# Second attention: the scores computed once, scaled by rows and turned, in place of a second pass of scores

## The reference

```python
qkv = data @ W_qkv + b_qkv
q = qkv[:, :, :DIM].reshape(n, l, H, HD)      # k, v alike; H=16, HD=64
scores = jnp.einsum('nqhd,nkhd->nhqk', q, k)
attention = jax.nn.softmax(scores / jnp.sqrt(jnp.float32(HD)), axis=3)
out = jnp.einsum('nhql,nlhd->nqhd', attention, v).reshape(n, l, DIM)
return out @ W_out + b_out
```

## Time and profile before

| | |
|---|---|
| median of 3 runs | 3018.5 us (3016.71 to 3020.96) |
| span of the profiled execution | 3025.9 us (its time beside the span is not recorded) |
| TensorE busy | 2770.4 us (92%) |
| VectorE busy | 2107.9 us (70%) |
| ScalarE busy | 1731.9 us (57%) |
| GpSimd busy | 1752.1 us (58%) |
| chain that ended last | PE 31%; DVE 4%; POOL 4%; issue 4%; ACT 2% |

### The profile page before, as it was taken

One profiled execution on the slowest core, in us unless ns is written; L12 is line 12 of the kernel. 1 busy time (PEld: TensorE's weight loads), 2 busy tenths in 40 slices (PEclk: granted clock), 3 DMA queues, 4 the chain that ended last, 5 costly groups with the idle time before them and its releaser, 6 DMA issues. The chain is left out here.

```text
span 3025.9 us, 50008 instructions
## 1 busy us (share of the span) xinstructions
PE 2770.4 (92%) x17716; PEld 1938.1 (64%) x17716; DVE 2107.9 (70%) x4508; ACT 1731.9 (57%) x3340; POOL 1752.1 (58%) x1540
## 2 busy tenths in 40 slices
PE   7999999999999999989994787999999999999376
PEld 6995565656656565648883674666666666665276
DVE  5667777777777777666776435877877778777632
ACT  5665777776776767676772343544544545445142
POOL 0004989898898989891110573555555555555067
PEclk9999999999999999989996798999999999999588
DMA  3015444444544545420002331000000000000033
GB/s 101 1 58 129 119 117 117 115 114 109 130 106 113 123 106 131 105 71 5 23 15 67 72 60 33 2 5 5 9 5 6 5 9 5 5 6 9 28 84 50
DMA packets 146695, 179.65 MB, mean 59 GB/s; under 512 B 31571, under 2 KB 76176, under 8 KB 145936
## 3 DMA queue, kind: packets, MB, share of 16 engines
q1 hardware_dynamic: 132368, 165.72, 21.7%
q0 software_dynamic: 14080, 10.73, 2.7%
HBM read 56.51 MB, written 17.72 MB: 25 GB/s over the span
## 5 line engine op out<-in xcount | busy, mean ns | idle before, releaser
L1982 POOL TENSOR_TENSOR arena<-arena 128x512 f32<-128x512 f32 x1152 | 1447.0, 1284 | 565.7 <-ACT arena L1325 450.8
L1605 DVE TENSOR_REDUCE top<-psum 128x1 f32<-128x512 f32 x1536 | 974.6, 677 | 196.0 <-PE psum L917 123.6
L1325 ACT ACTIVATE arena<-psum 128x512 f32<-128x512 f32 x1536 | 840.8, 600 | 240.7 <-PE psum L917 141.3
L909 PE MATMUL psum<-stack 96*128 96x512 f32 (+1 forms) x2048 | 627.5, 426 | 16.5 <-ACT arena L1325 9.3
L960 PE MATMUL psum<-arena,values 128*32 128x512 f32 (+1 forms) x3072 | 477.6, 597 | 3.4 <-ACT arena L1325 3.4
L909 PEld LDWEIGHTS psum<-stack 96*128 96x128 f32 (+1 forms) x2048 | 344.0, 191 | 198.1 <-DVE top L1605 87.7
L960 PEld LDWEIGHTS psum<-arena,values 128*32 128x32 f32 (+1 forms) x3072 | 134.0, 119 | 290.0 <-issue 284.8
L917 PE MATMUL psum<-stack 64*128 64x512 f32 x2048 | 292.5, 399 | 11.8 <-DVE top L1605 5.6
L1951 POOL TENSOR_SCALAR rstd<-mv 128x4 f32<-128x4 f32 x56 | 13.0, 233 | 480.0 <-DVE mv L1466 478.1
L1636 DVE RECIPROCAL psum<-psum 128x128 f32<-128x128 f32 x256 | 228.5, 934 | 25.3 <-PE psum L999 25.3
L917 PEld LDWEIGHTS psum<-stack 64*128 64x128 f32 x2048 | 200.4, 184 | 59.0 <-issue 26.0
(11 more groups left out here) (189 smaller groups left out, 3895.3 us busy)
## 6 DMA issues: line engine op xcount, KB each, us to landing
stack<-halves SPq DMA_DIRECT2D x768, 128.0 KB, 2.3
qk_ring<-qk_split SPq DMA_DIRECT2D x64, 256.0 KB, 2.9
v_ring<-v_split SPq DMA_DIRECT2D x32, 256.0 KB, 3.0
tokens<-xn SPq DMA_DIRECT2D x16, 256.0 KB, 2.4
arena<-in_wg SPq DMA_DIRECT2D x16, 256.0 KB
arena<-in_wu SPq DMA_DIRECT2D x16, 256.0 KB
arena<-in_wd SPq DMA_DIRECT2D x16, 256.0 KB
wqkv<-in_w_qkv SPq DMA_DIRECT2D x2, 1536.0 KB, 9.5
```

The costliest lines, as they stand in the source:

```text
L909: return T_.matmul(bk, st[0:k, side, h, cols], st[0:k, 1 - side, h, :], start=True, stop=True)
L1325: S_.activation(prob[l][tile % N_PROB[l]][:, h, :], psum[:, bank[key], :], ACT.Exp, scale=scale).then_inc(released[bank[key]], 1)
L1605: give(V_.reduce_max(top[i][:, column:column + 1], psum[:, bank[key], :], AX.X), key)
L1982: ins = G_.tensor_tensor(to[:, h, :], old[:, h, :], prob[l][tile % N_PROB[l]][:, h, :], ALU.add)
```

## The change

In the second attention the scores are computed once, with queries in the partitions. VectorE takes each row's maximum, negated (`peak`); ScalarE reads the same bank again, takes the exponential with that maximum as its bias, writes 128x512 to SBUF (`by_query`, a ring of 12) and gives the row's sum (`row_sum`); the bank is free only then. VectorE inverts the sums of a tile (`shares`, four times a group, 128x2), GpSimd multiplies the rows by them in SBUF (eight times a group, 128x512). TensorE turns each 128x512 in four blocks of 128x128 into one bank (`turns`, eight times a group); ScalarE copies the first head's, VectorE the second's, into `by_key`. Then the values are weighed as before, and ScalarE's copy of the result goes directly where the output projection reads it. The second scores, the turned maxima with their DMAs, the additions on GpSimd, the sums by TensorE and the wide reciprocals and the product on VectorE are gone from this stage. The scale 1/8 goes into the query weights and biases once (`SHARP`). The result's bank comes from `other`. The due times of the stage are new. The first attention keeps its arithmetic and its due times.

```diff
-    dict(rows=(1.82, 1.82), queries=(0.75, 0.75), keys=(0.80, 0.80), values=(1.01, 1.01), maxima=(1.04, 1.48),
-         probs=(3.03, 3.47), last=(3.43, 4.05), sums=(4.38, 4.38), mix=(4.38, 4.83), out=(4.93, 4.97),
-         ahead=(-1.52, 0.45), route=(5.03, 10.53), ranks=(9.80, 10.86), keep=(10.00, 10.00)))
+    dict(project=(-0.110, 0.700), maxima=(0.980, 1.840), rows=(1.950, 1.950), probs=(2.250, 3.170),
+         last=(3.250, 3.370), mix=(3.940, 4.550), out=(4.530, 5.010), ahead=(-2.310, -0.790),
+         finish=(4.910, 4.910), settle=(5.570, 5.860)),
+    dict(queries=(0.660, 0.660), keys=(0.660, 0.730), values=(0.895, 0.914), maxima=(1.000, 1.750),
+         exps=(1.149, 1.808), shares=(1.341, 2.091), turns=(1.900, 2.650), last=(2.720, 3.000), out=(3.487, 3.487),
+         ahead=(-1.649, 0.537), route=(5.860, 10.512), ranks=(9.604, 10.454), keep=(9.996, 10.032)))
...
-                queue("probs", (l, n), heads * TILES_B, heads * TILES_B, n)
-                queue("sums", (l, n), 1, 1, n)
-            queue("mix", (l, n), 5, 5, n)
+                queue("exps", (n,), heads * TILES_B, heads * TILES_B, n)
+                queue("shares", (n,), TILES_B, TILES_B, n)
+                queue("turns", (n,), heads * TILES_B, heads * TILES_B, n)
...
+            elif i % HEADS[l] == 0:
+                for j in range(i, i + HEADS[l]):
+                    self.products.take(("score", l, n, j))
...
+    def exps(self, n):
+        for j in range(HEADS[1] * TILES_B):
+            self.products.give(("score", 1, n, j))
+            yield
+
+    def turns(self, n):
+        for j in range(HEADS[1] * TILES_B):
+            self.once(self.products, ("turn", n, j))
+            yield
...
+            def turns(n):
+                for i in range(n * HEADS[1] * TILES_B, (n + 1) * HEADS[1] * TILES_B):
+                    rows = by_query[i % N_ROWS]
+                    pe.wait_ge(scaled, i + 1)
+                    bk, done = place(("turn", *divmod(i, HEADS[1] * TILES_B)))
+                    turn(bk, [rows[:, kt * P:(kt + 1) * P] for kt in range(TILES_B)]).then_inc(done, 1)
+                    yield
...
-                        elif h == 0:
-                            both_heads([("prob", l, n, kt, head) for head in range(HEADS[l])],
-                                       [(hv[:, k, cols], hv[:, q, :]) for q, k in ((QH, KH), (QL, KH), (QH, KL))]
-                                       + [(ones_rows[n % N_STACK], top_rows[n % N_STACK])])
...
+                                  scale=SHARP if c < INNER else 1.0).then_inc(qkv_rounded, 1)
...
+            def exps(n):
+                for j in range(HEADS[1] * TILES_B):
+                    i, key = n * HEADS[1] * TILES_B + j, ("score", 1, n, j)
+                    qt, h = divmod(j, HEADS[1])
+                    if i >= N_ROWS:
+                        act.wait_ge(*rows_turned(i - N_ROWS))
+                    else:
+                        act.wait_ge(*arena_free(1))
+                    act.wait_ge(peaked, i + 1)
+                    S_.activation(by_query[i % N_ROWS], psum[:, bank[key], :], ACT.Exp, bias=peak[n % 2][:, qt, h:h + 1],
+                                  accum_out=row_sum[n % 2][:, qt, h:h + 1]).then_inc(released[bank[key]], 1)
+                    yield
+
...
+            def turns(n):
+                if n >= 2:
+                    act.wait_ge(*tile_weighed(1, n - 2, TILES_B - 1))
+                else:
+                    act.wait_ge(*arena_free(1))
+                for j in range(HEADS[1] * TILES_B):
+                    qt, h = divmod(j, HEADS[1])
+                    if h == 0:
+                        key = ("turn", n, j)
+                        act.wait_ge(*written(key))
+                        S_.activation(by_key[n % 2][:, :, h, qt * P:(qt + 1) * P],
+                                      psum[:, bank[key], :].rearrange("p (t q) -> p t q", t=TILES_B),
+                                      ACT.Copy).then_inc(released[bank[key]], 1)
+                    yield
...
-                S_.activation(weighted[l][n % 2], psum[:, bk, :], ACT.Copy).then_inc(released[bk], 1)
+                S_.activation(mixed[1][:, g, :] if l else weighted[n % 2], psum[:, bk, :], ACT.Copy).then_inc(released[bk], 1)
...
+                    if l:
+                        qt, h = divmod(j, HEADS[l])
+                        V_.reduce_max(peak[i][:, qt, h:h + 1], psum[:, bank[key], :], AX.X, negate=True).then_inc(peaked, 1)
+                    else:
+                        give(V_.reduce_max(top[i][:, j:j + 1], psum[:, bank[key], :], AX.X), key)
...
+            def shares(n):
+                for qt in range(TILES_B):
+                    dve.wait_ge(*read(("score", 1, n, HEADS[1] * qt + HEADS[1] - 1)))
+                    V_.reciprocal(row_share[n % 2][:, qt, :], row_sum[n % 2][:, qt, :]).then_inc(inverted_sums, 1)
+                    yield
...
+            def turns(n):
...
+                        key = ("turn", n, j)
+                        dve.wait_ge(*written(key))
+                        give(V_.tensor_copy(by_key[n % 2][:, :, h, qt * P:(qt + 1) * P],
+                                            psum[:, bank[key], :].rearrange("p (t q) -> p t q", t=TILES_B)), key)
...
-                    for q in range(TILES_B):
-                        c = slice(q * P, (q + 1) * P)
-                        done = tick(V_.reciprocal(psum[:, bank[key], c], psum[:, bank[key], c]))
-                        yield
...
-                    give(V_.tensor_tensor(mixed[l][:, g, :], weighted[l][i], psum[:, bank[key], :], ALU.mult), key)
...
+            def shares(n):
+                for qt in range(TILES_B):
+                    at = n * TILES_B + qt
+                    pool.wait_ge(inverted_sums, at + 1)
+                    for h in range(HEADS[1]):
+                        rows = by_query[(at * HEADS[1] + h) % N_ROWS]
+                        G_.tensor_scalar(rows, rows, row_share[n % 2][:, qt, h:h + 1], None, ALU.mult).then_inc(scaled, 1)
+                    yield
...
-                        for h in range(HEADS[l]):
-                            Y_.dma_start(
-                                top_rows[s][64 * h + r:64 * h + r + 1, :].rearrange("a (t q) -> a t q", t=TILES_B).bitcast(fp32),
-                                part[h * TILES_B:(h + 1) * TILES_B, :].bitcast(fp32)).then_inc(max_rows[s], 16)
```

More of the change, by code:

```diff
@@ L56 @@
 C_WIDTH = C_EMPTY + SLOT_ROWS
+SHARP = float(WIDTH[1]) ** -0.5
 PER_ROW = P // EXPERTS
@@ L221, in __init__ @@
                      project=self.project, maxima=self.maxima, rows=self.rows, probs=self.probabilities,
-                     last=self.last, sums=self.sums, mix=self.mix, out=self.out, finish=self.finish, settle=self.settle, ahead=self.ahead, fold=self.fold, experts1=self.experts1)
+                     exps=self.exps, turns=self.turns, last=self.last, sums=self.sums, mix=self.mix, out=self.out, finish=self.finish, settle=self.settle, ahead=self.ahead, fold=self.fold, experts1=self.experts1)
         play(order, parts)
@@ L286, in maxima @@
     def maxima(self, l, n):
[L287 to L291, removed]
-                yield
+        for i in range(HEADS[l] * TILES_B):
+            if l == 0:
+                self.once(self.products, ("score", l, n, i))
+            elif i % HEADS[l] == 0:
[10 more added lines that the diff above has]
+            yield
     def rows(self, l, n):
-        self.once(self.products if l else self.other, ("top", l, n))
+        self.once(self.other, ("top", l, n))
         yield
@@ L300, in probabilities @@
             for h in range(HEADS[l]):
-                if l == 0:
-                    self.once(self.products, ("prob", l, n, kt, h))
-                elif h == 0:
-                    for head in range(HEADS[l]):
-                        self.once(self.products, ("prob", l, n, kt, head))
+                self.once(self.products, ("prob", l, n, kt, h))
                 yield
-            if kt == 2 and l == 0:
+            if kt == 2:
                 self.mixed.take(("o", l, n))
@@ L311, in last @@
     def last(self, l, n):
-        ring = self.products if l else self.mixed
+        ring = self.other if l else self.mixed
         if l:
@@ L1137, in _ @@
             play(order, dict(prepare0=prepare0, route=route, ahead=ahead, compute0=compute0, project=project,
-                             maxima=maxima, rows=rows_of_maxima, probs=probabilities, last=last_tiles, sums=sums_of, mix=mix,
+                             maxima=maxima, rows=rows_of_maxima, probs=probabilities, turns=turns, last=last_tiles, sums=sums_of, mix=mix,
                              out=project_out, fold=fold, experts1=experts1))
@@ L1324, in probabilities @@
                         act.wait_ge(*written(key))
-                        S_.activation(prob[l][tile % N_PROB[l]][:, h, :], psum[:, bank[key], :], ACT.Exp,
+                        S_.activation(prob[tile % N_PROB][:, h, :], psum[:, bank[key], :], ACT.Exp,
```

(11 more changed lines are left out.)

222 lines of the change are left out of this document (108 added, 114 removed).

## The result

Four runs of each kernel: 3030.98 us (3029.03 to 3031.42) after, 3018.86 (3016.71 to 3020.96) before, ratio 1.0043 [1.0029, 1.0057]. The change makes the kernel 12.1 us slower; forecast were 67.

What follows compares the result with a forecast made beforehand. The prediction took TensorE's queue to bound the second attention, 13.62 us a group. Groups +53, helpers' once-a-batch work +16 and ends -2 summed to +67 us, giving 3085 us; 8-in-10 range 3010 to 3160.

Steps and rivals of the forecast that it cites:

- The removed 4.67 us: TensorE, per group of the second attention: second scores 3.66, sums 0.90 and turned maxima 0.11 us go away.
- The group, +53 said: Second attention: a group takes 14.45 us instead of 13.62, 0.83 more; over 64 groups +53 us.
- the ten changes at 2.1 us: TensorE's array changes its division ten times a group instead of three, costing 2.1 us (1.9 to 2.4).
- Turn-to-pair: TensorE's change of division from a turn to a head pair, four times a group at 0.25 us.
- pair-to-turn: TensorE's change of division from a head pair to a turn, three times a group, taken as 0.17 us.
- faster: Rival: changes of division at turns cost 0.08 us, removed and added work decide; 2990 us, chance 0.15.
- These stay: The 11.9 us a batch costs beyond its groups (output projection, turned inputs, logits) were said to remain.
- +16 for the helpers' other work: VectorE and ScalarE operations done once a batch delay a bank in rounds without slack: 2 us a batch, +16 us.
- The ends, -2 said: Filling and emptying the second attention's pipeline, shorter by 1.5 groups: -2 us (-8 to +5).
- free up to 1.7 us: GpSimd's scaling, taken as 1.0 us, has half a group before its turn and costs nothing up to 1.7 each.
- The clock: Rival: TensorE's clock falls because turns do not count as busy; +223 us, about 3300 us, chance 0.03.
- Work only: Rival: TensorE's stalls vanish as ScalarE and VectorE run ahead, 13.85 us a group; 3031 us, chance 0.13.

Runs made afterwards that it cites:

- e6: The changed kernel with each head's score products over the whole array, two changes of division a group instead of ten: 3082.1 us, ratio to before 1.0222.
- e12: The changed kernel with the once-a-batch work given the due times of the kernel before: 3055.8 us, ratio to before 1.0090.
- e2: The changed kernel without GpSimd's scaling by the row sums: 3015.3 us, ratio to before 0.9993.
- e7: The changed kernel; in the last group alone VectorE scales the second head's rows, GpSimd the first's: 3023.0 us, ratio to before 1.0022.
- e5: The kernel before with one of the four wide reciprocals of each group in the second attention: 3017.5 us, ratio 1.0002.
- e9: The kernel before with once-a-batch work (standardised inputs, logits, ranks) moved out of the stretch of head pairs: 3043.0 us, ratio 1.0050.
- e11: As e10, with the once-a-batch work and one reciprocal of a group moved as well: 3023.3 us, ratio to before 0.9988.
- e13: The kernel before with only ScalarE's standardising and VectorE's ranks moved out of the stretch of head pairs: 3024.6 us, ratio 0.9989.
- e8: The changed kernel with other due times only, seven changes of division a group instead of ten: 3023.0 us, ratio to before 1.0027.
- e10: The changed kernel with e8's order, and VectorE scales two of eight blocks a group, four in the last: 3006.3 us, ratio to before 0.9933.

## Why the prediction was right or wrong

**Direction, and what happens inside a plain group: right.** The kernel got slower as forecast. The removed 4.67 us are replaced by 3.52 us of turns, by changes of division and by waits, and TensorE stays the bound. Four turned blocks cost 0.44 us as said (2.27 against 2.26 in e6), the copy 0.68 (said 0.65), two exponentials and a copy on ScalarE 2.06 (2048.63 to 2050.69 in e12, with no wait between; said 2.17), the waits 0.55 (said 0.6).

**The group, +53 said, +31 measured: a size.** The term is the ten changes at 2.1 us. Turn-to-pair was priced 0.25 from one place with a turn of 65 columns, and pair-to-turn 0.17, together 0.42 a round; the clean round has 0.35 for the two, and e6 gives 0.17 a change on average. TensorE's own group is 14.14 - 0.55 = 13.6 us, not 13.9, so the ten changes took 1.8 us. The waits, 0.55 for 0.6, make the small rest. The rival "faster" had asked for under 0.13 a change.

**"These stay", and +16 for the helpers' other work: the step that failed, 42 us of the 55 by which the sum was off.** It was argued from total slack. What decides is the place in a helper's queue: in e12 1.64 us of ScalarE ahead of an exponential delay TensorE by up to 1.64, and with the due times of the change TensorE waits 0.3 us in 800 at these turns, not 19.4. The earlier trace rows held the sign of it, 11.9 us a batch of which the projection is 7.1; I did not ask what the other 4.8 were, and they were partly such waits, open to removal by the due times that the change edits. e12 shows that those due times carry the gain: without them the excess is 11.5, not 8.5. Of the 42 us, 16 are delays by the helpers' other work that did not come, and 14 to 20 are the due times by e12's time and stage; the rest is open, in part because 8 times a middle batch counts the first and the last batch too high.

**The ends, -2 said, +7 measured.** GpSimd's scaling takes 1.565 us; I took 1.0 and gave 1.284 as the upper bound, since an operation with two full operands took that. The bound was wrong: the form with one full operand is the slower one here. The prediction's own limit (free up to 1.7 us) nearly held in the body (0.12 us a group by e2), but not at the end, where nothing lies beside it. The Trainium skill (GPSIMD Engine Reference, Engine selection), cited in the prediction, has a one-input operation at roughly line rate and a two-input one about twice as slow as on VectorE. Here the scaling, whose only full operand is one, is the slower of the two on GpSimd (1.565 us against 1.284), and VectorE does it in 0.49.

**The clock.** That rival was wrong for the body: 1.00 over 800 us with 32 turned blocks in each 14.1 us. At the stage's end the level did fall, to 0.54, after the waits of 0.5 to 0.9 us between short turns, and cost about 2.9 us in one weighing; e7 removed it. A wait by itself does not settle it: behind one of 2.89 us the last projection of the kernel before took 7.41 us, and behind one of 2.90 that of e5, the same instructions, took 9.37. The Trainium skill (TensorE: Matmul & The Clock Gate, PE-mode transpose) says that a turn does not count as busy the same way as a product. Mixed with pairs and weighings no run here shows a loss by it, and at the end turns and waits came together, so the two aren't told apart.

**Work only** (3031 us, chance 0.13) has the right number by luck: it let the waits vanish, which stayed at 0.55 a group, and knew nothing of the gain per batch or the loss at the end.

## What to carry to other kernels

When a change trades products for turns, count how often the array's division changes (0.17 us each here), not only the columns. Work that comes once a batch belongs where no bank waits behind it in the helper's queue; its place was worth up to 3 us a batch, where the reading of the row sums costs 8 x 0.27. Such a place is not easy to find: e9, e11 and e13 each met a new wait elsewhere. A helper at 90% of its time cost 0.12 us a group in the body with the order of the change, 3 us once at the end, and some 3 us a batch with another order (e8). A better order and a quarter of the helper's work given to an engine with room (e10) together turned the loss of 0.4% into a gain of 0.7%; most of it came with the second (e8 alone: a loss of 0.3%).

## What the hardware showed that was not expected

GpSimd scales 128x512 by a column in 1.565 us, slower than its addition of two such operands (1.284); VectorE does the same scaling in 0.49.

Where both engines read and write SBUF alone, they can slow each other, and in two places it is the operation that started second that pays. The comparison L1492 of the kernel before takes 1.43 us in the six batches in which an addition of GpSimd began 0.12 to 0.14 us ahead of it (above: 2302.27 against 2302.42), and 0.43 with GpSimd idle. In e7 the order is the other way: VectorE's scaling begins 0.06 us ahead and keeps its 0.49, and GpSimd's takes 1.86 to 2.11 (four of four) instead of 1.565:

```profile
2789.42 0.49 DVE L1671 TENSOR_SCALAR arena<-arena,row_tables 128x512 f32<-128x512 f32 x1
...
2789.48 1.86 POOL L2066 TENSOR_SCALAR arena<-arena,row_tables 128x512 f32<-128x512 f32 x1 [0.53 <-DVE row_tables L1667]
```

In e10 the order of the starts does not tell it. VectorE's scaling begins 0.75 us into GpSimd's and keeps its 0.48, and it is GpSimd's that takes longer (1.70 for the first of the two):

```profile
1934.00 0.48 DVE L1681 TENSOR_SCALAR by_query<-by_query,row_tables 128x512 f32<-128x512 f32 x1
...
1933.25 3.24 POOL L2078 TENSOR_SCALAR by_query<-by_query,row_tables 128x512 f32<-128x512 f32 x2 [3.75 <-DVE row_tables L1676]
```

So that the two engines get in each other's way is shown by these rows, and by what rule one of them pays is not; no run was made for this alone.
